# 16-head cross attention: the scores of four heads on four quarters of TensorE's rows

## The chip, the cores and the metric

The kernel runs on one core of a Trainium2 chip. The metric is the device time of one execution in microseconds (us), lower is better. TensorE is PE in the profile (its weight loads are PEld), VectorE is DVE, ScalarE is ACT, GpSimd is POOL, and SP issues most DMAs.

## The reference

A decoder of four layers, each of them self attention, cross attention and feed-forward, in float32, on x of 8 batches x 100 rows x 256 channels. Three of the four cross attentions (layers 0, 1 and 3) have 16 heads of 16 channels and attend to a context of 361 rows. Cut to what matters:

```python
def _L3_xattn_ref(x, context, Wq, Wk, Wv, Wo, bo):      # 16 heads of 16 channels
    q = (x @ Wq.T).reshape(B, Qlen, HEADS, HEAD_DIM).transpose(0, 2, 1, 3)
    k = (context @ Wk.T).reshape(B, KVlen, HEADS, HEAD_DIM).transpose(0, 2, 1, 3)
    v = (context @ Wv.T).reshape(B, KVlen, HEADS, HEAD_DIM).transpose(0, 2, 1, 3)
    scores = jnp.einsum('bhqd,bhkd->bhqk', q, k) / scale
    attn = jax.nn.softmax(scores, axis=-1)
    out = jnp.einsum('bhqk,bhkd->bhqd', attn, v)
    ...
    return out @ Wo.T + bo
```

Layer 0 adds biases, rotary embedding and a key mask, layer 1 biases and a gate on the values.

## The kernel before

`build` emits the sublayers one after another with a barrier of all engines between them. `cross_attn16` is called three times: as `l0x` (with rotation and key mask), `l1x` (with the gate) and `l3x`. Tiles carry that prefix (`l1x_pr`). Layer 2 has another function with four heads, which is not touched.

A stage of `cross_attn16` first projects keys, values and queries of all batches. `kt` holds the keys transposed: 128 partitions are 8 heads of 16 channels, and the 16 heads fill two such blocks (`KC = 2`). Then comes the score loop over 32 quads (8 batches x 4 quads of 4 heads), written out by hand on every engine; the order in the code is the order of each engine's queue:

- PE, step n: transposes of heads 0 and 1 of quad n-1 (`turn`, L1078); the scores of quad n (`score`, L1068), one PSUM bank of `wide` for each head; transposes of heads 2 and 3 of quad n-1; in every fourth step, each at another place, one of `back` (L1098), `turn_y` (L1104), `project_y` (L1110), which finish a batch; then the product with the values of quad n-2 (`weigh`, L1089).
- DVE, step n: copy of head 0 of quad n-1 out of PSUM (`copy_pt`, L1340); the lowest score of each row for quad n (`lowest`): in l1x and l3x two reduces over two heads each (L1356), in l0x one pass for each head that also adds the mask (L1350); copy of head 2 of quad n-1; in some steps `divide` or `add`.
- ACT, step n: copy of head 1 of quad n-1 (L1200), exponentials of heads 0 and 1 of quad n (L1209), copy of head 3 of quad n-1, exponentials of heads 2 and 3.

`turned` has two banks: the transposes of head 0 of quad n wait until the copy of head 2 of quad n-1 has read bank 0. Head i of a score waits until bank i of `wide` has been read: by ACT's exponential of the quad before (l1x, l3x), or by DVE's pass (l0x).

A head's 16 channels are fewer than the partitions that a matmul takes, so the queries are masked: POOL writes `qm` (L1250), which holds copies of the queries in which all channels but one head's are zero, for two batches by turns. Before, a head's score contracts 64 partitions, `t` chooses the half, and `qm` has four masked copies. The host permutes the columns of the query and key weights by `SLOT_HEAD`, so that the heads 0, 1, 2, 3 of a quad lie in the halves 0, 1, 0, 1.

The trace shows each float32 matmul as two weight loads and two matmuls: 128 head scores of a stage are 256 matmuls.

Of the kernel before, what the change touches and what calls it, by code (L numbers as in the profile page):

```python
# [17 lines left out]
B, S, E = 8, 100, 256  # L18
P = 128
KC = E // P  # L20
SKV = 361
# [8 lines left out]
ALU = mybir.AluOpType  # L30
# [884 lines left out]
                walk(dve, front, step, finish)  # L915


SLOT_HEAD = [8 * m + 4 * (j // 2) + 2 * (j % 2) + t for m in range(KC) for t in range(2) for j in range(4)]


@sublayer
def cross_attn16(net, name, rope=False, biases=False, key_mask=False, gate=False, load=False):
# [3 lines left out]
    nc, dram = net.nc, net.dram  # L926
# [6 lines left out]
    with ExitStack() as ctx:  # L933
        def sb(n, shape, dt=F32):
            return ctx.enter_context(nc.sbuf_tensor(name + "_" + n, shape, dt))

        w = {n: sb(n, [P, KC, E]) for n in ("wk", "wv", "wq", "wo")}
        pairs = [(w["wk"][:], dram[name + "_wk"])]
# [8 lines left out]
        if rope:  # L947
# [2 lines left out]
            pairs += [(swap[:], dram["rope_swap"]), (cos[:], dram["rope_cos"]), (sin[:], dram["rope_sin"])]  # L950
            kraw, qraw = sb("kraw", [P, 2, KC, SKV]), sb("qraw", [P, KC, HALF * S])
            ksin, qsin = sb("ksin", [P, KC, SKV]), sb("qsin", [P, KC, HALF * S])
        headmask = sb("headmask", [P, 4])
        pairs += [(w["wq"][:], dram[name + "_wq"]), (headmask[:], dram["headmask4"]), (w["wo"][:], dram[name + "_wo"])]
        bo = None
        if name + "_bo" in dram:
            bo = sb("bo", [S, E])
# [7 lines left out]
        xn = sb("xn", [S, B, E])  # L965
        xt = sb("xt", [P, KC, B, S])
        qt = sb("qt", [P, KC, B, S])
        qm = sb("qm", [P, 2, KC, 4, S])
        kt = sb("kt", [P, B, KC, SKV])
        v1 = sb("v1", [CH, B, NCH, H, V])  # L970
        nmx = sb("nmx", [S, 2, Q])
# [15 lines left out]
        wide, turned, summed, side = net.wide, net.turned, net.summed[:, 0, :], net.summed[:, 1, :]  # L987
# [19 lines left out]

        def rows_of(c):
            return CH if c < NCH - 1 else LAST

        def slot_of(g, i):
            return g // 2, i % 2, 2 * (g % 2) + i // 2

        with nc.Block() as block:
            @block.sync
            def _(sp):
                load_weights(sp, net, pairs[:1], sem["loaded"])
                if load:
                    net.context.load(sp, net)
                load_weights(sp, net, pairs[1:], sem["loaded"])  # L1020

            @block.tensor
            def _(pe):
# [36 lines left out]
                def score(n):  # L1060
                    b, g = n // NQ, n % NQ
                    if g == 0:
                        pe.wait_ge(sem["qm_ready"], b + 1)
                    for i in range(Q):
                        m, t, j = slot_of(g, i)
                        if n >= 1:
                            pe.wait_ge(sem["m_ready" if key_mask else "p_ready"], Q * (n - 1) + i + 1)
                        pe.matmul(wide[0:S, i, 0:SKV], qm[64 * t:64 * t + 64, b % 2, m, j, :], kt[64 * t:64 * t + 64, b, m, :],  # L1068
                                  start=True, stop=True).then_inc(sem["s_psum"], 1)

                def turn(n, heads):
# [69 lines left out]
                for n in range(QUADS + 2):  # L1141
                    if 1 <= n <= QUADS:
                        turn(n - 1, (0, 1))
                    if n < QUADS:
                        score(n)
                    if 1 <= n <= QUADS:
                        turn(n - 1, (2, 3))
                    b = n // NQ - 1
                    if n % NQ == 2 and b >= 0:
                        back(b)  # L1150
                    elif n % NQ == 3 and b >= 0:
                        turn_y(b)
                    elif n % NQ == 0 and b >= 1:
                        project_y(b - 1)
                    if n >= 2:
                        weigh(n - 2)
# [81 lines left out]
            @block.gpsimd  # L1238
            def _(pool):
                pool.memset(pr[:, :, SKV:PADKV], 0.0).then_inc(sem["pad_ready"], 1)  # L1240
                pool.memset(v1[:, :, :, :, D:V], 0.0)
                pool.drain()
                pool.memset(v1[:, :, :, :, D:D + 1], 1.0).then_inc(sem["ones_ready"], 1)
                pool.wait_ge(sem["loaded"], n_loaded)
                for b in range(B):
                    pool.wait_ge(sem["q_ready"], KC * (b // HALF) + KC)
                    if b >= 2:
                        pool.wait_ge(sem["s_psum"], H * (b - 1))
                    for m in range(KC):
                        last = pool.tensor_tensor(qm[:, b % 2, m], qt[:, m, b, :].unsqueeze(1).broadcast_to([P, 4, S]),  # L1250
                                                  headmask[:].unsqueeze(2).broadcast_to([P, 4, S]), ALU.mult)
                    last.then_inc(sem["qm_ready"], 1)

            @block.vector
# [1763 lines left out]
def build(nc, dram):  # L3018
    with ExitStack() as ctx:
        net = Net(nc, ctx, dram)  # L3020
        with ExitStack() as kept:
            net.context = Context(net, kept, "ctxt")
            front(net)
        l3_attn(net)
        net.context = Context(net, ctx, "ctxt3")
        cross_attn16(net, "l3x", load=True)
        l3_ffn(net)
        store(net)


def front(net):
    setup(net)
    l0_attn(net)
    cross_attn16(net, "l0x", rope=True, biases=True, key_mask=True)
    l0_ffn(net)
    l1_attn(net)
    cross_attn16(net, "l1x", biases=True, gate=True)
    l1_ffn(net)
    l2_attn(net)
    cross_attn(net, "l2x", 4, mask=("query_mask", U8))  # L3040
    l2_ffn(net)


def _layouts(a):

    def wide(w):
        return w.reshape(-1, P, w.shape[-1]).transpose(1, 0, 2)

    def col(b):
        return b.reshape(-1, P).T  # L3050

    d = {"x": a["x"], "ident": np.eye(P, dtype=np.float32)}
    d["causal"] = np.where(np.arange(S)[:, None] < np.arange(S)[None, :], np.float32(NEG), np.float32(0))
    d["ctxt"] = a["ctx_1024"].transpose(0, 2, 1).reshape(B, KC, P, SKV).transpose(0, 2, 1, 3)
    for D in (16, 64):
        d[f"headmask{D}"] = (np.arange(P)[:, None] // D == np.arange(P // D)[None, :]).astype(np.float32)
    d["headmask4"] = ((np.arange(P)[:, None] % 64) // 16 == np.arange(4)[None, :]).astype(np.float32)
    slots = (np.array(SLOT_HEAD)[:, None] * 16 + np.arange(16)[None, :]).reshape(-1)
    for n in ("q", "k", "v"):
        d["l0a_w" + n] = wide(a["L0_attn_w_" + n].reshape(-1, E).T)  # L3060
    d["l0a_wo"] = wide(a["L0_attn_w_o"])
    for k, n in (("l0x", "L0_xattn"), ("l1x", "L1_xattn")):
        for m in "qkvo":
            d[f"{k}_w{m}"] = wide(a[f"{n}_W{m}"][:, slots] if m in "qk" else a[f"{n}_W{m}"])
        for m in "qk":
            d[f"{k}_b{m}"] = col(a[f"{n}_b{m}"][slots])
        for m in "vo":
            d[f"{k}_b{m}"] = a[f"{n}_b{m}"]
    wkv = a["L2_xattn_Wkv"]
    for m, w in (("q", a["L2_xattn_Wq"]), ("k", wkv[:E]), ("v", wkv[E:]), ("o", a["L2_xattn_Wout"])):  # L3070
        d["l2x_w" + m] = wide(w.T)
    for m in "qkvo":
        d["l3x_w" + m] = wide(a["L3_xattn_W" + m].T[:, slots] if m in "qk" else a["L3_xattn_W" + m].T)
    d["l3x_bo"] = a["L3_xattn_bo"]
    d["key_mask"] = a["mask_Bx1x1xS2_if1"].reshape(B, SKV)
    bits = np.zeros((B, S, -(-SKV // 4) * 4), np.bool_)
    bits[:, :, 0:SKV] = a["mask_BxSxS2_bk0"]
    d["query_mask"] = bits.view(np.int32)

    D = 16  # L3080
    r = np.arange(P) % D
    inv = (1.0 / np.float32(10000.0) ** (np.arange(0, D, 2, dtype=np.float32) / np.float32(D))).astype(np.float32)
    angle = (np.arange(SKV, dtype=np.float32)[None, :] * inv[r % (D // 2)][:, None]).astype(np.float32)
    d["rope_cos"], d["rope_sin"] = np.cos(angle), np.sin(angle)
    swap = np.zeros((P, P), np.float32)
    for p in range(P):
        lower = r[p] < D // 2
        swap[p + D // 2 if lower else p - D // 2, p] = -1.0 if lower else 1.0
    d["rope_swap"] = swap

    rows = np.minimum(np.arange(PADKV), SKV - 1)
    d["energy"] = a["ctxb_2048x8"][:, rows].reshape(B * NCH, CH, 8).transpose(1, 0, 2)
    more_layouts(a, d, wide, col)
    return {k: np.ascontiguousarray(v) for k, v in d.items()}
# [13 lines left out]
```

## Time and profile before

| | |
|---|---|
| three runs | 2272.12, 2280.46, 2282.67 us; median 2280.46 us |
| the profiled execution | 2281.18 us, span of its instructions 2279.2 us |
| mean granted clock of TensorE | 0.846 |
| score loop of l0x, first to last score | 175.5 us |
| score loop of l1x, first to last score | 129.8 us |
| score loop of l3x, first to last score | 127.7 us |

The span is the time from the first to the last instruction; the execution's own time is 2.0 us longer. The three score loops together are 433.0 us of 2279.2 us; all else in the kernel is not touched by the change, apart from the size of one small weight tile and of the masked queries. A granted clock of 1.00 is 2.4 GHz and 0.50 is 1.2 GHz; values between are means over a stretch in which both levels occur.

### The profile page before, as it was taken

Reading aid. Unit: us, or ns where it says so; the run is one execution under the profiler, and the core shown is the slowest. Engines: PE = TensorE matmul, PEld = TensorE weight load, DVE = VectorE, ACT = ScalarE, POOL = GpSimd, SP = SyncE. Lnnn points to the kernel's source line nnn. Section 1 sums busy time; section 2 is a strip of 40 time slices with the busy share of each in tenths; the row PEclk is TensorE's granted clock in tenths of the full one; section 3 lists DMA queues with packets and bytes.
Section 4 is the critical chain, followed back from the end, with each engine's and each line's share of the span. In section 5 each row is a group of like instructions: output and inputs, shape, how many; then the busy total and the mean of one; then the engine's idle time right before and its main releaser. Section 6 shows DMA issues by size and latency. Waiting matters only on the chain. (4 is left out here: it accounts for less than half of the span.)

```text
span 2279.2 us, 30680 instructions
## 1 busy us (share of the span) xinstructions
PE 1711.9 (75%) x10556; PEld 1224.0 (54%) x10556; DVE 1069.9 (47%) x2341; ACT 728.8 (32%) x1482; POOL 331.8 (15%) x247
## 2 busy tenths in 40 slices
PE   4998688779789799879996177728925572199978
PEld 4887455546478566568885055517712220066643
DVE  2544465655543457520000623320028899736665
ACT  1222135543288256422221122212213300026630
POOL 0000100000021101031112100020022994101000
PEclk9999798988855899889998578958968775599989
DMA  3000100001000000143653100044120000100010
GB/s 142 1 0 6 46 1 1 1 9 35 26 1 0 25 1 2 63 146 114 209 190 111 43 22 14 7 176 149 55 68 0 0 0 0 73 0 2 2 45 15
DMA packets 41358, 102.73 MB, mean 45 GB/s; under 512 B 9789, under 2 KB 27690, under 8 KB 36404
## 3 DMA queue, kind: packets, MB, share of 16 engines
q1 hardware_dynamic: 29194, 56.85, 7.2%
q0 software_dynamic: 7216, 39.63, 5.2%
q10 hardware_dynamic: 4830, 4.71, 0.7%
q8 instruction: 70, 1.15, 0.2%
q14 instruction: 48, 0.39, 0.1%
HBM read 89.28 MB, written 11.88 MB: 44 GB/s over the span
## 5 line engine op out<-in xcount | busy, mean ns | idle before, releaser
L2602 PE MATMUL wide<-l3a_qk,ident 100*100 100x512 f32 x144 | 80.3, 714 | 51.1 <-POOL l3a_qk L2692 50.3
L2030 PE MATMUL summed<-l1f_pack,l1f_hidden 128*100 128x256 f32 x480 | 107.3, 382 | 2.9 <-ACT l1f_hidden L2079 2.9
L2164 DVE TENSOR_TENSOR l1f_out<-summed,l1f_b 100x512 f32<-100x512 f32 x15 | 10.4, 692 | 187.8 <-PE summed L2030 187.8
L2030 PEld LDWEIGHTS summed<-l1f_pack,l1f_hidden 128*100 128x100 f32 x480 | 78.9, 167 | 27.9 <-ACT l1f_hidden L2079 5.9
L1209 ACT ACTIVATE l0x_pr<-l0x_sc,l0x_nmx 100x361 f32<-100x361 f32 x128 | 75.1, 593 | 56.8 <-DVEq L1352 55.9
L1350 DVE CUSTOM_DVE_ANT_0 l0x_sc<-wide,l0x_words 100x361 f32<-100x361 f32 x128 | 68.4, 534 | 50.6 <-PE wide L1068 33.2
L2079 ACT ACTIVATE l1f_hidden<-wide,l1f_pack 128x200 f32<-128x200 f32 x120 | 48.9, 426 | 135.0 <-PE wide L2024 82.8
L1078 PE MATMUL turned<-ident,l0x_pr 100*121 100x100 f32 x384 | 62.8, 305 | 35.5 <-DVE l0x_pt L1340 22.3
L2692 POOL TENSOR_TENSOR l3a_qk<-l3a_cw,l3a_score 100x1024 f32<-100x1024 f32 x36 | 86.6, 2438 | 4.3 <-DVE l3a_score L2756 4.3
L1078 PEld LDWEIGHTS turned<-ident,l0x_pr 100*121 100x121 f32 x384 | 52.0, 208 | 63.9 <-ACT l0x_pr L1209 42.3
L2024 PE MATMUL wide<-l1f_rt,l1f_pack 128*128 128x200 f32 x480 | 83.9, 333 | 0.7 <-ACT l1f_rt L2089 0.7
L2024 PEld LDWEIGHTS wide<-l1f_rt,l1f_pack 128*128 128x128 f32 x480 | 81.6, 190 | 2.4 <-issue 1.5
L2602 PEld LDWEIGHTS wide<-l3a_qk,ident 100*100 100x100 f32 x144 | 27.1, 198 | 102.5 <-POOL l3a_qk L2692 55.4
L1209 ACT ACTIVATE l1x_pr<-wide,l1x_nmx 100x361 f32<-100x361 f32 x128 | 65.2, 567 | 47.1 <-DVE l1x_nmx L1356 47.1
L1209 ACT ACTIVATE l3x_pr<-wide,l3x_nmx 100x361 f32<-100x361 f32 x128 | 65.1, 567 | 44.7 <-DVE l3x_nmx L1356 44.7
L1356 DVE TENSOR_REDUCE l1x_nmx<-wide 100x2 f32<-100x722 f32 x64 | 55.4, 905 | 26.3 <-PE wide L1068 26.3
L1356 DVE TENSOR_REDUCE l3x_nmx<-wide 100x2 f32<-100x722 f32 x64 | 55.3, 905 | 24.3 <-PE wide L1068 24.3
L1068 PE MATMUL wide<-l0x_kt,l0x_qm 64*100 64x361 f32 x256 | 58.4, 584 | 5.2 <-DVE l0x_kt L1290 5.2
L1078 PEld LDWEIGHTS turned<-ident,l1x_pr 100*121 100x121 f32 x384 | 46.3, 187 | 29.6 <-issue 17.9
L1078 PEld LDWEIGHTS turned<-ident,l3x_pr 100*121 100x121 f32 x384 | 45.5, 184 | 29.3 <-issue 17.5
L1078 PE MATMUL turned<-ident,l1x_pr 100*121 100x100 f32 x384 | 56.5, 284 | 5.9 <-DVE l1x_pt L1340 5.4
L1078 PE MATMUL turned<-ident,l3x_pr 100*121 100x100 f32 x384 | 55.8, 281 | 6.7 <-DVE l3x_pt L1340 5.6
(523 smaller groups left out, 3931.6 us busy)
## 6 DMA issues: line engine op xcount, KB each, us to landing
l2f_w<-l2f_w_dram SPq DMA_DIRECT2D x16, 1024.0 KB
ctxt<-ctxt_dram SPq DMA_DIRECT2D x4, 1083.0 KB, 8.1
l1f_sorted_x<-l1f_zeros SPq DMA_DIRECT2D x15, 200.0 KB
l1f_rows<-l1f_sorted_x SPq DMA_DIRECT2D x15, 200.0 KB
l1f_sorted_y<-l1f_out ACTq DMA_DIRECT2D x15, 200.0 KB
l2x_ctxt<-ctxt_dram SPq DMA_DIRECT2D x8, 361.0 KB
l0f_w<-l0f_w_dram SPq DMA_DIRECT2D x18, 128.0 KB
l1f_shared<-l1f_shared_dram SPq DMA_DIRECT2D x1, 2052.0 KB
```

Source lines behind the costliest of these rows:

```text
L1068: pe.matmul(wide[0:S, i, 0:SKV], qm[64 * t:64 * t + 64, b % 2, m, j, :], kt[64 * t:64 * t + 64, b, m, :], start=True, stop=True).then_inc( ...
L1078: last = pe.transpose(turned[0:CH, i % 2, c * S:(c + 1) * S], pr[:, h % 8, c * CH:(c + 1) * CH], net.ident[0:S, 0:S])
L1209: act.activation(pr[:, h % 8, 0:SKV], src, ACT.Exp, bias=nmx[:, n % 2, i:i + 1], scale=-1.0).then_inc(sem["p_ready"], 1)
L1350: dve.tensor_tensor_reduce(sc[:, i, :], wide[0:S, i, 0:SKV], bias[:, b, :], 1.0, 3e38, ALU.add, ALU.min, nmx[:, n % 2, i:i + 1])
L1356: dve.tensor_reduce(nmx[:, n % 2, 2 * pair:2 * pair + 2], wide[0:S, 2 * pair:2 * pair + 2, 0:SKV], X_AX, ALU.min).then_inc(sem["m_ready"], 2)
L2024: last = pe.matmul(wide[:, f % 4, 0:CR], w1_of(w, k, f), cols(k), start=k == 0, stop=k == KC - 1)
L2030: last = pe.matmul(banks[0:S, c, 0:E], hidden[:, f, c * S:(c + 1) * S], w2_of(w, f), start=f == 0, stop=f == FC - 1)
L2079: act.activation(hidden[:, f, :], wide[:, f % 4, 0:CR], ACT.Gelu, bias=b1_of(w, f)).then_inc(read, 1)
L2164: dve.tensor_tensor(out[:, slot], summed[0:S, :, 0:E], b2[:, slot, :].unsqueeze(1).broadcast_to([S, RT, E]), ALU.add).then_inc(sem["y_read ...
L2602: last = pe.matmul(wide[0:S, 2 * (t % 2) + half, :], net.ident[0:S, 0:S], ring[:, n % RING, half * HALF:(half + 1) * HALF], start=u == 0, ...
L2692: pool.tensor_tensor(ring[:, n % RING, :].rearrange("s (h c) -> s h c", h=H), cw[:, u, :].rearrange("s (h c) -> s h c", h=H), score[:, n, ...
```

## The change

The scores of the four heads of a quad are placed on four quarters of the array's rows. A head's score now contracts 32 partitions (two heads' channels), heads 0 to 3 of a quad take the partitions 0-31, 32-63, 64-95 and 96-127, and the masked queries need two copies instead of four. `SLOT_HEAD`, the host's permutation, follows. Number, order, waits and increments of PE's instructions stay as they are; so do the output banks.

```diff
-SLOT_HEAD = [8 * m + 4 * (j // 2) + 2 * (j % 2) + t for m in range(KC) for t in range(2) for j in range(4)]
+SLOT_HEAD = [8 * m + 4 * t + i for m in range(KC) for i in range(4) for t in range(2)]
...
-        headmask = sb("headmask", [P, 4])
-        pairs += [(w["wq"][:], dram[name + "_wq"]), (headmask[:], dram["headmask4"]), (w["wo"][:], dram[name + "_wo"])]
+        headmask = sb("headmask", [P, 2])
+        pairs += [(w["wq"][:], dram[name + "_wq"]), (headmask[:], dram["headmask2"]), (w["wo"][:], dram[name + "_wo"])]
...
-        qm = sb("qm", [P, 2, KC, 4, S])
+        qm = sb("qm", [P, 2, KC, 2, S])
...
-        def slot_of(g, i):
-            return g // 2, i % 2, 2 * (g % 2) + i // 2
...
-                        m, t, j = slot_of(g, i)
                         if n >= 1:
                             pe.wait_ge(sem["m_ready" if key_mask else "p_ready"], Q * (n - 1) + i + 1)
-                        pe.matmul(wide[0:S, i, 0:SKV], qm[64 * t:64 * t + 64, b % 2, m, j, :], kt[64 * t:64 * t + 64, b, m, :],
+                        pe.matmul(wide[0:S, i, 0:SKV], qm[32 * i:32 * i + 32, b % 2, g // 2, g % 2, :], kt[32 * i:32 * i + 32, b, g // 2, :],
                                   start=True, stop=True).then_inc(sem["s_psum"], 1)
...
-                        last = pool.tensor_tensor(qm[:, b % 2, m], qt[:, m, b, :].unsqueeze(1).broadcast_to([P, 4, S]),
-                                                  headmask[:].unsqueeze(2).broadcast_to([P, 4, S]), ALU.mult)
+                        last = pool.tensor_tensor(qm[:, b % 2, m], qt[:, m, b, :].unsqueeze(1).broadcast_to([P, 2, S]),
+                                                  headmask[:].unsqueeze(2).broadcast_to([P, 2, S]), ALU.mult)
...
-    d["headmask4"] = ((np.arange(P)[:, None] % 64) // 16 == np.arange(4)[None, :]).astype(np.float32)
+    d["headmask2"] = ((np.arange(P)[:, None] % 32) // 16 == np.arange(2)[None, :]).astype(np.float32)
```

## Rows read from the trace of the kernel before

**Rows 1.** The page of the whole execution: span, then busy time (share) x instructions of each engine.

```profile
span 2279.2 us, 30680 instructions
...
PE 1711.9 (75%) x10556; PEld 1224.0 (54%) x10556; DVE 1069.9 (47%) x2341; ACT 728.8 (32%) x1482; POOL 331.8 (15%) x247
```

**Rows 2.** Stretches: score loops of l0x, l1x, l3x. Length, busy (x) of PE, PEld, DVE, ACT, POOL, PEclk.

```profile
317.70:493.20 175.50, 141.59 (x1376) 93.98 (x1376) 105.53 (x336) 96.49 (x197) 9.98 (x12) 0.88 0.01 2
808.70:938.50 129.80, 124.37 (x1376) 84.12 (x1376) 88.59 (x149) 84.01 (x197) 9.98 (x12) 0.97 0.01 2
2040.80:2168.50 127.70, 121.48 (x1374) 82.83 (x1374) 88.38 (x149) 83.67 (x197) 9.98 (x12) 1.00 0.01 2
```

**Rows 3.** Groups by line, score loop of l1x: busy us, mean ns, idle before and releaser.

```profile
L1356 DVE TENSOR_REDUCE l1x_nmx<-wide 100x2 f32<-100x722 f32 x64 | 55.4, 905 | 26.3 <-PE wide L1068 26.3
L1068 PE MATMUL wide<-l1x_kt,l1x_qm 64*100 64x361 f32 x256 | 48.8, 501 | 2.5 <-issue 2.5
...
L1250 POOL TENSOR_TENSOR l1x_qm<-l1x_qt,l1x_headmask 128x400 f32<-128x400 f32 x12 | 10.0, 852 | 115.9 <-PE wide L1068 115.9
```

**Rows 4.** Timeline of l1x, PE, two quads: start us, us, what, count, idle before.

```profile
859.16 1.46 PE L1068 MATMUL wide<-l1x_kt,l1x_qm 64*100 64x361 f32 x8
...
861.26 1.03 PE L1110 MATMUL summed<-l1x_wo,l1x_yt 128*100 128x256 f32 x4
...
863.68 1.46 PE L1068 MATMUL wide<-l1x_kt,l1x_qm 64*100 64x361 f32 x8
865.07 0.88 PE L1078 MATMUL turned<-ident,l1x_pr 100*121 100x100 f32 x6
865.88 0.72 PE L1089 MATMUL summed<-l1x_pt,l1x_v 121*32 121x100 f32 x24
866.93 0.85 PE L1078 MATMUL turned<-ident,l1x_pr 100*121 100x100 f32 x6 [0.33 <-DVE l1x_pt L1340]
867.71 0.55 PE L1068 MATMUL wide<-l1x_kt,l1x_qm 64*100 64x361 f32 x2
```

**Rows 5.** Timeline of l1x, DVE, the quad from 863.68.

```profile
864.68 1.73 DVE L1356 TENSOR_REDUCE l1x_nmx<-wide 100x2 f32<-100x722 f32 x2 [0.73 <-PE wide L1068]
866.32 0.46 DVE L1340 COPY l1x_pt<-turned 121x300 f32<-121x300 f32 x1
```

**Rows 6.** Timeline of l1x, ACT, the quad from 863.68.

```profile
865.62 1.01 ACT L1209 ACTIVATE l1x_pr<-wide,l1x_nmx 100x361 f32<-100x361 f32 x2 [1.42 <-DVE l1x_nmx L1356]
...
866.83 1.02 ACT L1209 ACTIVATE l1x_pr<-wide,l1x_nmx 100x361 f32<-100x361 f32 x2
```

**Rows 7.** Timeline of PE cut down to 863.8 to 864.0, then to 864.10 to 864.15.

```profile
863.68 0.55 PE L1068 MATMUL wide<-l1x_kt,l1x_qm 64*100 64x361 f32 x2
...
863.68 0.85 PE L1068 MATMUL wide<-l1x_kt,l1x_qm 64*100 64x361 f32 x4
```

**Rows 8.** Timeline of l0x, PE, the end of the quad from 392.00.

```profile
396.65 0.85 PE L1078 MATMUL turned<-ident,l0x_pr 100*121 100x100 f32 x6 [1.72 <-DVE l0x_pt L1340]
397.42 0.55 PE L1068 MATMUL wide<-l0x_kt,l0x_qm 64*100 64x361 f32 x2
```

**Rows 9.** Timeline of l0x, DVE, the quad from 392.00: first head, last copy.

```profile
392.99 0.53 DVE L1350 CUSTOM_DVE_ANT_0 l0x_sc<-wide,l0x_words 100x361 f32<-100x361 f32 x1 [0.73 <-PE wide L1068]
...
396.03 0.47 DVE L1340 COPY l0x_pt<-turned 121x300 f32<-121x300 f32 x1 [0.19 <-issue]
```

**Rows 10.** Stretches: two of l0x, then two quads of l1x; columns as in rows 2.

```profile
420.20:423.40 3.20, 3.20 (x22) 2.16 (x22) 2.33 (x9) 2.14 (x5) 0.00 (x0) 0.50 0.00 0
389.50:420.00 30.50, 23.35 (x273) 15.98 (x273) 19.03 (x62) 17.81 (x37) 1.66 (x2) 1.00 0.00 1
812.89:817.98 5.09, 4.54 (x21) 2.63 (x21) 2.41 (x4) 2.84 (x7) 0.00 (x0) 0.69 0.00 0
867.71:871.80 4.09, 4.09 (x49) 2.87 (x48) 3.15 (x7) 3.00 (x8) 0.00 (x0) 1.00 0.02 4
```

**Rows 11.** Timeline of l1x, DVE, second reduce of the quad from 812.89.

```profile
815.77 0.91 DVE L1356 TENSOR_REDUCE l1x_nmx<-wide 100x2 f32<-100x722 f32 x1 [0.29 <-PE wide L1068]
```

## The prediction, made before the changed kernel ran

> **What bounds the kernel now.** I read the page first: PE is busy for 75% of the span and DVE for 47%, but that is a mean over twelve sublayers [rows 1]. So I cut out the three stretches that the change touches, first to last score of each stage [rows 2]. PE is busy for 121.48 of 127.70 us in l3x (95%), for 124.37 of 129.80 in l1x, for 141.59 of 175.50 in l0x. By that alone PE bounds l1x and l3x, and the score matmuls, 48.8 us there [rows 3], are a third of it. But a stretch that is nearly full of PE work can still be set by a loop through other engines, so the next view is the timeline of one quad.
>
> In l1x the quad that begins at 863.68 lasts until 867.71, 4.03 us [rows 4]. Most quads of l1x and l3x last that long. PE has one pause in it: 0.33 us before the transposes at 866.93, and what ends it is DVE's copy of line 1340, not a score. Followed back on DVE [rows 5]: the copy runs from 866.32 to 866.78, directly behind two reduces that start at 864.68 and hold DVE for 1.73 us; these start when the scores of heads 0 and 1 are there, 1.00 us after the first score. So the loop is: score begins, +1.00 first reduce, about +2.64 copy of head 2, about +3.25 next transposes of heads 0 and 1, about +4.03 next score. Nothing in it asks when heads 2 and 3 are scored: they are needed by the second reduce alone, which starts some 0.82 us after the first (864.68 + 1.73 - 0.91, with 905 ns a reduce [rows 3]), at +1.82. The scores have all ended by +1.46.
>
> Two of four quads have more PE work and no pause. The one from 859.16 has the output projection of 1.03 us and lasts 4.52 us [rows 4]; there are six of these in each of l1x and l3x. The one from 867.71 has the transposes of line 1098 and lasts 4.09 us with PE busy for all of it [rows 10]; seven in each. Only in these does PE set the time.
>
> In l0x a quad takes 397.42 - 392.00 = 5.42 us at full clock, PE pauses for up to 1.72 us, again ended by the copy of line 1340 [rows 8], and DVE is in four single passes from 392.99 to the copy at 396.03 [rows 9]. The loop has the same form, with a longer DVE part.
>
> **The change part by part.** *The scores.* Cut to a narrow window, the trace has two matmuls in flight at 863.8, and four that span 0.85 us when the second passes have begun [rows 7]: the halves of the rows really work at once, and two heads take 0.85 us. The whole quad takes 1.46, so the second pair of heads adds 0.61. If four quarters work at once, as two halves do, the quad takes 0.85 us: PE gains 0.61 us in each of 96 quads, 58.6 us of PE time. No row shows four row quarters. The nearest are the products of line 1089, where four heads lie on four quarters of the columns: 24 matmuls in 0.72 us, 30 ns each [rows 4], where six transposes of the same 100 columns on the whole array take 0.88 us, 147 ns each. So four small matmuls at once are usual for this array, and I take 0.85. The bounds are 1.46 (still by pairs) and, as the worst, four that share what two have now, so that all four end at 1.46 and heads 0 and 1 too.
>
> Where does the 0.61 go? In the usual quad it becomes pause. Heads 0 and 1 are ready at +0.85 as before, the reduces start at +1.00, and every later step of the loop stays. Gain: nothing; the cover is the loop through DVE. In the quads in which PE sets the time the gain is cut by two things. One is the loop's 4.03 us. The other is a wait that so far is hidden: heads 2 and 3 wait for ACT to have read their banks. ACT's last exponential of the quad ends at 866.83 + 1.02 = 867.85 [rows 6], 0.14 us after the next score has begun; with the step to PE I put heads 2 and 3 at +0.2 at the earliest. Before they began at +0.69, so it cost nothing; now the scores end at about 1.05, and PE gains 0.41. The quad with the projection goes from 4.52 to 4.11: 6 x 0.41 = 2.5 us a stage. The other goes from 4.09 to the loop's 4.03: 7 x 0.06 = 0.4 us. That is 2.9 us a stage, 5.8 us for l1x and l3x. Behind the waiting score of head 2 stand the transposes of heads 2 and 3 and the values' product; nobody waits for these before the next transposes at +3.25. A single case more: in the first two quads of l1x the clock is partly at 1.2 GHz, the second reduce waits for the scores, 0.29 us [rows 11], and that goes: 0.6 us for two. Sum so far: -6.4 us.
>
> In l0x the scores of heads 2 and 3 are wanted still later, since DVE takes heads one by one, and no quad at full clock is set by PE. Gain: nothing.
>
> *The masked queries.* POOL's multiplication, 852 ns each, has half the elements. POOL waits for PE 115.9 us in the loop of l1x [rows 3], so this is worth nothing, and would be worth nothing if it were slower. The smaller mask's DMA and the permuted weights change no wait.
>
> *The clock.* This is the only part that can cost. In l0x the mean granted clock is 0.88 [rows 2], so a share of 2 x 0.12 = 0.24 of the 175.5 us, 42 us, is at 1.2 GHz; one such stretch stands in [rows 10]. What PE did before it fell was pausing. The stage has 31 quads from first to last score; at 5.42 us they would be 168.0, it is 175.5, so the lower level costs 7.5 us, 0.18 for each us at it. The change adds 0.61 us of pause to every quad of l0x, some 19 us in all. I take 20 us more at the lower level, x 0.18 = 3.6 us; the bounds are none, and twice as much as now, 7.5 us. That four heads at once shorten slow quads in which PE is full works against it; at most all 7.5 us of today come back. In l1x and l3x the pause grows too: PE would be busy for about 121.48 - 32 x 0.41 = 108.4 of 125 us in l3x, 13% idle. The long stretch of l0x from 389.50 to 420.00 has PE idle for 7.15 of 30.50 us, 23%, and stays at 2.4 GHz throughout [rows 10]. By that row l1x and l3x keep their clock, and I take nothing. The Trainium skill says (TensorE: Matmul & The Clock Gate, Part 1) that the gate follows how busy the array has been lately, which is a rule against this change: a faster score leaves the array idle more. The trace agrees in l0x, and whether the rule bites in l1x and l3x is the first rival below.
>
> Sum: -5.8 - 0.6 + 3.6 = -2.8 us. The profiled execution took 2281.18 us (span 2279.2 and 2.0 around it), which lies 0.7 above the median of the three runs. 2281.18 - 2.8 = 2278.4; I say 2278.
>
> **The rivals.** *The clock falls in l1x and l3x as well (slower).* Place: the score loops of both. For it: pauses grow from 0.33 to over 0.7 us in the usual quad, and l0x shows that pauses bring the clock down. Against: the row with 23% idle. Price: the l1x quad from 812.89 lasted 5.09 us at a mean clock of 0.69 [rows 10], which is 0.62 of it or 3.2 us at the lower level, for 1.06 us more than 4.03: 0.34 a us. If both loops spend a quarter of their 257 us there, as l0x does, it is 64 x 0.34 = 22 us, with 7.5 in l0x and -6.4: +23, 2304 us. It decides from about 50 us at the lower level in the two.
>
> *The four quarters share, and the first heads come late (slower).* Heads 0 and 1 end at 1.46 and no longer at 0.85; each loop gets 0.61 longer, 96 x 0.61 = 58.6 us, 2340 us. Against: halves do not slow each other, column quarters do not.
>
> *The array still takes them two at a time.* Nothing but POOL's work changes: 2281 us.
>
> *PE is the bound after all.* 96 x 0.61 us come off, 2223 us. For it: 95% busy in l3x. Against: the pause ended by DVE's copy in the usual quads. The Trainium skill (TensorEngine Tiling (Array Packing), PSUM Bottleneck) warns that a faster TensorE can leave the copies out of PSUM as the limit, and the trace agrees that DVE, which reads these scores, is already in the loop.
>
> *l0x gets its slow quads back.* The clock does not fall oftener there, and the 7.5 us of excess come off with the 6.4: 2267 us.
>
> **How the numbers follow.** Chances: the forecast 0.64, clock in l1x and l3x 0.12, shared quarters 0.05, pairs as before 0.06, PE the bound 0.05, l0x back 0.08. The forecast's own range is 2271 to 2288: all the bounds of its terms (-6.4 with -7.5 is the last rival; -6.4 with +7.5 is 2282, and the three runs spread by 10 us). To leave out no more than 2 in 10, the range goes to the clock rival above and to the l0x rival below: 2266 to 2304. A change within 0.5%, 11.4 us, is about what a measurement of this kernel cannot tell from none; the forecast and the pairs fall there (0.70), slower are the clock and the sharing (0.17), faster PE as bound and l0x (0.13).
>
> **What would show it.** The scores of a quad span 0.85 to 1.05 us and no longer 1.46. In l1x and l3x the first reduce still starts 1.00 us after the score, usual quads stay at 4.03 us, and PE's pause before the transposes grows to 0.7 to 0.9 us, ended by the copy of line 1340. The projection's quad takes 4.1 us. The loops last about 126 us (l1x) and 125 us (l3x), that of l0x 179 us at a clock near 0.83. I am wrong if the first reduce starts later or earlier than +1.00, if the clock of l1x or l3x is under 0.95, or if usual quads are shorter than 4.0 us.

## The result, and the profile after

The changed kernel takes 2300.8 us (median of five runs, 2294.95 to 2309.5), the kernel before 2280.46 us: ratio 1.0093, 95% interval 1.006 to 1.0126. It is slower, by about 20 us. The time lies inside the range that the prediction gave, but the prediction said "no change", and a small gain at that; what happened comes nearest to its first rival, the clock that falls in l1x and l3x too, though not for that rival's reason nor in its sizes. A second measurement gave 1.0090 (1.0058 to 1.0122). One of the nine executions of l0x_whole below, 3577 us at a granted clock of 0.975 against 2251 to 2261 us of the other eight, is in a slow state and is left out of its ratio.

First the page of the changed kernel, then its three score loops (l0x, l1x, l3x, first to last score; columns as in [rows 2]):

```profile
span 2298.8 us, 30680 instructions
...
PE 1711.9 (74%) x10556; PEld 1236.0 (54%) x10556; DVE 1067.5 (46%) x2341; ACT 729.5 (32%) x1482; POOL 316.2 (14%) x247
...
PEclk9999877777855779889998578959968775598979
```

```profile
315.90:503.30 187.40, 149.45 (x1377) 103.14 (x1378) 105.26 (x336) 96.43 (x197) 6.00 (x12) 0.70 0.01 1
820.00:952.40 132.40, 118.92 (x1377) 84.65 (x1377) 87.62 (x149) 83.85 (x197) 6.00 (x12) 0.90 0.01 2
2053.90:2187.00 133.10, 120.95 (x1375) 85.82 (x1375) 87.65 (x149) 83.94 (x197) 6.00 (x12) 0.88 0.01 2
```

PE's busy time is the same to a tenth, 1711.9 us, and that is the first hint: the scores need less of it at full clock, so the rest must have become slower. The loops went from 175.5 to 187.4, from 129.8 to 132.4 and from 127.7 to 133.1 us, 19.9 us together, and the span grew by 19.6: all of it is there. The granted clock went from 0.88 to 0.70, from 0.97 to 0.90 and from 1.00 to 0.88.

Where the clock is at 2.4 GHz, the trace does what the prediction said. PE in l1x, a quad with the projection and the usual quad behind it, which answer to [rows 4]:

```profile
858.93 1.05 PE L1064 MATMUL wide<-l1x_kt,l1x_qm 32*100 32x361 f32 x8
...
860.62 1.03 PE L1106 MATMUL summed<-l1x_wo,l1x_yt 128*100 128x256 f32 x4
...
863.04 0.96 PE L1064 MATMUL wide<-l1x_kt,l1x_qm 32*100 32x361 f32 x8
863.93 0.88 PE L1074 MATMUL turned<-ident,l1x_pr 100*121 100x100 f32 x6
864.74 0.72 PE L1085 MATMUL summed<-l1x_pt,l1x_v 121*32 121x100 f32 x24
866.29 0.85 PE L1074 MATMUL turned<-ident,l1x_pr 100*121 100x100 f32 x6 [0.83 <-DVE l1x_pt L1336]
867.07 0.56 PE L1064 MATMUL wide<-l1x_kt,l1x_qm 32*100 32x361 f32 x3
```

The scores take 1.05 and 0.96 us (before 1.46). The projection's quad lasts 863.04 - 858.93 = 4.11 us (before 4.52), the usual one 4.03 us as before, and PE's pause before the transposes grew from 0.33 to 0.83 us, still ended by DVE's copy. DVE shows why, as in [rows 5]:

```profile
864.04 1.73 DVE L1352 TENSOR_REDUCE l1x_nmx<-wide 100x2 f32<-100x722 f32 x2 [0.73 <-PE wide L1064]
865.68 0.46 DVE L1336 COPY l1x_pt<-turned 121x300 f32<-121x300 f32 x1
```

The reduces start at 864.04, 1.00 us behind the first score, exactly as before. Scoring heads 2 and 3 earlier gives the loop nothing.

What the prediction did not have is this. Three stretches of the loop of l3x, then one of l1x and one of l0x:

```profile
2053.90:2058.10 4.20, 2.54 (x21) 1.55 (x22) 2.20 (x3) 2.23 (x5) 0.00 (x0) 1.00 0.00 0
2058.30:2088.80 30.50, 30.32 (x225) 21.17 (x227) 15.46 (x25) 15.63 (x36) 1.00 (x2) 0.50 0.01 2
2089.00:2187.00 98.00, 87.70 (x1135) 62.92 (x1123) 69.79 (x121) 65.88 (x157) 5.00 (x10) 1.00 0.01 2
823.00:849.50 26.50, 25.59 (x184) 17.69 (x187) 12.45 (x20) 12.69 (x30) 1.00 (x2) 0.50 0.00 1
315.94:360.40 44.46, 35.51 (x258) 24.17 (x258) 22.69 (x72) 20.67 (x41) 1.00 (x2) 0.52 0.01 1
```

l3x begins at 2.4 GHz, PE is busy for 2.54 of the first 4.20 us, and then 30.5 us are at 1.2 GHz, after which the clock comes back and stays. In the kernel before, the loop of l3x is at 2.4 GHz throughout. l1x has 26.5 us of the same, and the first 44.46 us of l0x have a mean clock of 0.52, so nearly all of them are at 1.2 GHz, there with pauses of PE. One of the slow quads of l3x, PE and then the first reduce on DVE:

```profile
2067.62 1.54 PE L1064 MATMUL wide<-l3x_kt,l3x_qm 32*100 32x361 f32 x8
2069.09 1.54 PE L1074 MATMUL turned<-ident,l3x_pr 100*121 100x100 f32 x6
2070.56 1.23 PE L1085 MATMUL summed<-l3x_pt,l3x_v 121*32 121x100 f32 x24
2071.72 1.54 PE L1074 MATMUL turned<-ident,l3x_pr 100*121 100x100 f32 x6
2073.20 0.94 PE L1064 MATMUL wide<-l3x_kt,l3x_qm 32*100 32x361 f32 x4
```

```profile
2069.29 1.73 DVE L1352 TENSOR_REDUCE l3x_nmx<-wide 100x2 f32<-100x722 f32 x2 [1.70 <-PE wide L1064]
```

The quad lasts 5.58 us, PE has no pause at all in it, and yet the clock stays down for some five such quads. In the kernel before, the quad from 812.89 in l1x was at the lower level too [rows 10], but the clock was back before its end. Why a PE without a pause didn't get its clock back is what the experiments had to explain.

### The profile page after: what moved, and what is told of

It reads as the page before. It is cut to its first block and busy times, and to the rows that moved or that the text cites. A ratio compares the mean times of both kernels' runs of the same rounds, so it can differ in the third digit from the quotient of the medians.

```text
span 2298.8 us, 30680 instructions
## 1 busy us (share of the span) xinstructions
PE 1711.9 (74%) x10556; PEld 1236.0 (54%) x10556; DVE 1067.5 (46%) x2341; ACT 729.5 (32%) x1482; POOL 316.2 (14%) x247
## 5 line engine op out<-in xcount | busy, mean ns | idle before, releaser
L1074 PE MATMUL turned<-ident,l0x_pr 100*121 100x100 f32 x384 | 76.8, 354 | 40.3 <-DVE l0x_pt L1336 24.5
L1074 PEld LDWEIGHTS turned<-ident,l0x_pr 100*121 100x121 f32 x384 | 64.2, 251 | 73.7 <-ACT l0x_pr L1205 48.8
L2160 DVE TENSOR_TENSOR l1f_out<-summed,l1f_b 100x512 f32<-100x512 f32 x15 | 10.4, 692 | 187.4 <-PE summed L2026 187.4
L1074 PEld LDWEIGHTS turned<-ident,l3x_pr 100*121 100x121 f32 x384 | 52.0, 207 | 39.3 <-issue 21.6
L1074 PEld LDWEIGHTS turned<-ident,l1x_pr 100*121 100x121 f32 x384 | 51.3, 205 | 40.1 <-issue 21.0
L1074 PE MATMUL turned<-ident,l1x_pr 100*121 100x100 f32 x384 | 62.2, 303 | 14.3 <-DVE l1x_pt L1336 12.6
L1074 PE MATMUL turned<-ident,l3x_pr 100*121 100x100 f32 x384 | 63.0, 306 | 13.1 <-DVE l3x_pt L1336 11.4
L2885 PE MATMUL wide<-l3f_we,l3f_xt 128*100 128x512 f32 x128 | 59.7, 621 | 1.2 <-DVE l3f_acc L2953 1.2
```

The source lines that it names most:

```text
L1074: last = pe.transpose(turned[0:CH, i % 2, c * S:(c + 1) * S], pr[:, h % 8, c * CH:(c + 1) * CH], net.ident[0:S, 0:S])
L2160: dve.tensor_tensor(out[:, slot], summed[0:S, :, 0:E], b2[:, slot, :].unsqueeze(1).broadcast_to([S, RT, E]), ALU.add).then_inc(sem["y_read ...
L2885: last = pe.matmul(wide[0:S, n, :], xt[:, k, b, :], we[:, k, n * 512:(n + 1) * 512], start=k == 0, stop=k == KC - 1)
```

## The experiments

Each kernel ran on one chip together with the kernel before, whose median was between 2263 and 2282 us from chip to chip; so ratios to the kernel before are what to compare. The three numbers of us are the score loops of one profiled execution, from the start of the first score to the start of the last, with the granted clock. Some expectations count to the end of the last score, 0.3 to 0.9 us more, and 2.0 us more where scores use 128 rows.

| kernel | ratio (95%) | l0x | l1x | l3x |
|---|---|---|---|---|
| before | 1 | 175.5 (0.88) | 129.8 (0.97) | 127.7 (1.00) |
| changed | 1.0093 (1.006 to 1.0126) | 187.4 (0.70) | 132.4 (0.90) | 133.1 (0.88) |
| changed_again | 1.0090 (1.0058 to 1.0122) | 190.3 (0.67) | 127.6 (0.96) | 133.1 (0.88) |
| fill_start | 1.0051 (1.0034 to 1.0067) | 187.2 (0.71) | 127.9 (0.98) | 124.7 (1.00) |
| fill_start_32 | 1.0144 (1.0116 to 1.0172) | 189.5 (0.68) | 135.7 (0.89) | 135.3 (0.89) |
| fill_128 | 0.9953 (0.9933 to 0.9973) | 170.6 (0.97) | 126.5 (0.99) | 124.7 (1.00) |
| fill_32 | 1.0497 (1.0468 to 1.0526) | 250.0 (0.54) | 144.7 (0.85) | 149.1 (0.82) |
| two_quarters | 1.0285 (1.0259 to 1.0312) | 202.5 (0.64) | 144.3 (0.86) | 151.1 (0.81) |
| l0x_quarters_only | 1.0084 (1.0063 to 1.0105) | 190.0 (0.67) | 132.0 (0.95) | 127.7 (1.00) |
| l0x_whole | 0.9955 (0.9936 to 0.9974) | 164.0 (0.99) | 132.0 (0.95) | 127.7 (1.00) |
| halves_fill | 0.9949 (0.9932 to 0.9966) | 170.1 (0.98) | 128.1 (1.00) | 127.8 (1.00) |
| whole_and_quarters | 0.9976 (0.9957 to 0.9995) | 164.1 (0.99) | 135.4 (0.86) | 133.1 (0.88) |
| l0x_whole_quarters | 0.9903 (0.9882 to 0.9924) | 164.2 (0.99) | 125.0 (1.00) | 124.6 (1.00) |

**Is it the clock? Dummies in the first quads.** `fill` emits dummy matmuls into columns of PSUM that nothing else uses, ahead of `weigh`; each is two instructions on the PE. They change no result.

```diff
+def fillers(name, n):
+    return {0: 8, 1: 6, 2: 3}.get(n, 0) if name != "l0x" else 0
...
+                def fill(n):
+                    for _ in range(fillers(name, n)):
+                        pe.matmul(summed[:, NQ * S:512], net.ident[0:128, :], ctxt[0:128, 0, 0, 0:512 - NQ * S], start=True, stop=True)
...
+                    fill(n)
                     if n >= 2:
                         weigh(n - 2)
```

> The changed kernel with dummy matmuls (two instructions of 112 columns each, whole array, into unused columns) in the first three steps of the score loops of l1x and l3x alone: 8, 6 and 3 of them. Clock theory: in the changed kernel both loops begin with some 27 and 31 us at 1.2 GHz, because PE pauses in the first quads; with the pauses filled the clock stays at 2.4 GHz, l1x goes from 132.4 to about 126 us, l3x from 133.1 to about 125 us, and the whole is about 14 us faster than the changed kernel: 2287 us. Rival (the four row quarters cost time by themselves, the clock is a by-product): the dummies change nothing or cost 2 to 4 us, 2301 to 2305 us. l0x stays at about 187 us in either.

Loops of fill_start:

```profile
312.40:499.60 187.20, 148.19 (x1374) 102.30 (x1374) 105.19 (x336) 96.38 (x197) 5.98 (x12) 0.71 0.01 1
815.20:943.10 127.90, 114.55 (x1411) 83.34 (x1411) 87.55 (x149) 83.53 (x197) 5.98 (x12) 0.98 0.01 2
2029.60:2154.30 124.70, 111.92 (x1411) 81.31 (x1411) 87.55 (x149) 83.44 (x197) 5.98 (x12) 1.00 0.01 2
```

PE executes 34 instructions more in each of l1x and l3x, and l3x gets 8.4 us shorter, 124.7 us; l1x goes to 127.9. The changed kernel and this one differ by 0.42% of the whole, 9 to 10 us; 14 were expected, of which 13 show in the profile. The intervals of the two ratios, 1.006 to 1.0126 and 1.0034 to 1.0067, just touch, so this pair alone doesn't settle the time of the whole; the last pair of kernels below does. In l3x the long slow stretch is no cost that four quarters have by themselves: with quarters and dummies the loop has none. The first quads of a stage have few or no transposes and products of earlier quads to do, and the stretch doesn't come when dummies on the whole array stand in for them. l0x is as slow as in the changed kernel, as expected.

**Dummies everywhere, on 128 rows and on 32.** 3 to 6 dummies in a step of l0x (8 in the first), up to 3 in a usual step of l1x and l3x; the second kernel is the same but for the rows.

```diff
-                        pe.matmul(summed[:, NQ * S:512], net.ident[0:128, :], ctxt[0:128, 0, 0, 0:512 - NQ * S], start=True, stop=True)
+                        pe.matmul(summed[:, NQ * S:512], net.ident[0:32, :], ctxt[0:32, 0, 0, 0:512 - NQ * S], start=True, stop=True)
```

> The changed kernel with dummy matmuls on the whole array in the pauses of all three score loops: 3 to 8 in a step of l0x, up to 3 in a usual step of l1x and l3x, more in their first steps. Clock theory: no stretch at 1.2 GHz in l1x and l3x (126 and 125 us), and few in l0x, whose quads go to their 5.42 us: 168 to 172 us instead of 187. Whole: 2265 to 2275 us, faster than both kernels. Rival (quarters cost by themselves): 2300 us or more, since the dummies only add work.

> As the kernel with dummies in all pauses, with the same number of dummies, columns and instructions, but each contracts 32 partitions and not 128. If the clock goes by how long the array is kept busy, whatever part of it works, this is as fast as the one with 128: 2265 to 2275 us. If it goes by how many rows of the array work, the dummies are worth a quarter: the clock stays low as in the changed kernel, and the dummies stretch the slow quads of l0x: 2295 to 2315 us.

Loops of fill_128, then of fill_32:

```profile
318.40:489.00 170.60, 143.52 (x1696) 112.90 (x1696) 104.83 (x336) 96.58 (x197) 5.98 (x12) 0.97 0.01 2
802.50:929.00 126.50, 123.58 (x1500) 93.27 (x1500) 87.54 (x149) 83.61 (x197) 5.99 (x12) 0.99 0.01 2
2014.00:2138.70 124.70, 122.36 (x1503) 92.20 (x1503) 87.60 (x149) 83.56 (x197) 5.99 (x12) 1.00 0.01 2
```

```profile
318.20:568.20 250.00, 247.60 (x1696) 187.44 (x1696) 105.64 (x336) 96.98 (x197) 5.99 (x12) 0.54 0.00 1
887.60:1032.30 144.70, 144.30 (x1500) 106.75 (x1500) 87.62 (x149) 84.27 (x197) 5.98 (x12) 0.85 0.01 2
2116.00:2265.10 149.10, 149.00 (x1500) 109.36 (x1500) 87.75 (x149) 84.35 (x197) 5.99 (x12) 0.82 0.01 2
```

The two execute the same number of instructions with the same columns. With 128 rows the kernel is faster than the one before by 0.47%, and l0x has a clock of 0.97. With 32 rows it is 5% slower, and in l0x PE is busy for 247.60 of 250.00 us at 1.2 GHz for nearly all of it (0.54). By PE's busy time the second kernel is the busiest of all, and it has the lowest clock. Of the size I had expected less, 1.006 to 1.015: I had not thought that l0x would stay down for the whole loop, where the dummies themselves take twice as long.

That objection, dummies that lengthen quads which are already slow, doesn't apply if they stand in the first three steps alone, before the clock falls:

> As the kernel with dummies in the first three steps of l1x and l3x alone, but each dummy contracts 32 partitions. It lies in pauses before the clock has fallen, so that it can't be blamed for lengthening slow quads as the dummies of 32 rows in all pauses could. If the clock goes by rows: the loops of l1x and l3x begin at 1.2 GHz as in the changed kernel, 132 to 136 us each, ratio 1.008 to 1.014. If by busy time alone: 128.4 and 125.1 us as with whole-array dummies, ratio 1.005.

```profile
826.30:962.00 135.70, 124.80 (x1408) 90.38 (x1408) 87.53 (x149) 83.75 (x197) 6.00 (x12) 0.89 0.01 2
2064.40:2199.70 135.30, 125.00 (x1408) 90.14 (x1408) 87.64 (x149) 83.81 (x197) 6.00 (x12) 0.89 0.01 2
```

Both loops have about the clock of the changed kernel and are 3.3 and 2.2 us longer than in it; the ratio, 1.0144, is at the upper end of what was expected. The first 6.9 us of the loop of l3x in three kernels, the one before, fill_start and fill_start_32, and then what follows in the third:

```profile
2040.80:2047.70 6.90, 4.84 (x30) 2.97 (x30) 4.30 (x6) 3.71 (x9) 0.00 (x0) 1.00 0.00 0
2029.60:2036.50 6.90, 6.90 (x58) 5.58 (x59) 4.30 (x6) 3.72 (x9) 0.00 (x0) 1.00 0.00 0
2064.40:2071.30 6.90, 6.90 (x56) 5.61 (x56) 4.30 (x6) 3.72 (x9) 0.00 (x0) 1.00 0.00 0
2071.50:2102.00 30.50, 30.50 (x232) 21.66 (x233) 13.55 (x22) 14.20 (x33) 1.00 (x2) 0.50 0.01 2
```

This is the cleanest comparison of all. Before the clock falls, PE is busy for all of the 6.90 us with either kind of dummy, and for only 4.84 us in the kernel before. With dummies of 32 rows the clock then falls and is down for 30.5 us in which PE has no pause; with dummies of 128 rows, and in the kernel before with its scores of 64 rows, it never falls in this loop. The dummies of 32 rows put the fall off, from 4.2 us after the first score in the changed kernel to 7, and don't prevent it. Between the two kernels with dummies only the dummies' rows differ. So PE's busy time doesn't decide: the clock followed how much of the array's rows worked.

**The scores themselves, with half the rows for the same time.** Heads 0 and 2 on one quarter, heads 1 and 3 on another: two scores run at a time, as with halves.

```diff
-SLOT_HEAD = [8 * m + 4 * t + i for m in range(KC) for i in range(4) for t in range(2)]
+SLOT_HEAD = [8 * m + 4 * (q // 2) + 2 * t + q % 2 for m in range(KC) for q in range(4) for t in range(2)]
...
-                        pe.matmul(wide[0:S, i, 0:SKV], qm[32 * i:32 * i + 32, b % 2, g // 2, g % 2, :], kt[32 * i:32 * i + 32, b, g // 2, :],
+                        q = 2 * (g % 2) + i % 2
+                        pe.matmul(wide[0:S, i, 0:SKV], qm[32 * q:32 * q + 32, b % 2, g // 2, i // 2, :], kt[32 * q:32 * q + 32, b, g // 2, :],
```

> Scores of 32 partitions as in the changed kernel, but heads 0 and 2 of a quad on one quarter of the rows and heads 1 and 3 on another, so that two work at a time: the array is busy with scores as long as in the kernel before (1.46 us a quad), with half the rows. If the clock goes by busy time alone, this is the kernel before again, 2280 us, mean clock 0.846. If it goes by rows, the clock is as low as in the changed kernel or lower and the quads in which PE sets the time are as long as before: 2300 to 2315 us, clock 0.81 to 0.82. The rival that something else in the change costs time (layout of heads, smaller masked queries) also expects about 2300 us, but then with the clock of the kernel before.

```profile
314.40:516.90 202.50, 188.56 (x1376) 124.77 (x1376) 106.14 (x336) 96.50 (x197) 5.99 (x12) 0.64 0.01 1
831.00:975.30 144.30, 140.01 (x1376) 94.53 (x1376) 89.08 (x149) 84.73 (x197) 5.98 (x12) 0.86 0.01 2
2064.70:2215.80 151.10, 147.30 (x1374) 98.99 (x1374) 89.23 (x149) 85.09 (x197) 5.99 (x12) 0.81 0.01 1
```

Against the kernel before, PE is busy longer and the clock is lower in every loop, 0.64, 0.86 and 0.81 against 0.88, 0.97 and 1.00: 2.85% slower, where I had expected 0.9 to 1.5%. In this kernel as in the changed one a head's 16 channels come with 16 zeroed ones, and with halves they come with 48. The zeros are useless arithmetic, but the clock was higher where they were worked through. The rows and columns of score work are the same here as in the changed kernel, and yet this one is slower still: a slow quad lasts longer, since two pairs of scores one after the other take longer than four scores at once.

```profile
2094.73:2101.50 6.77, 6.77 (x47) 4.46 (x46) 2.67 (x4) 3.15 (x7) 0.00 (x0) 0.50 0.01 2
```

It takes 6.77 us and no longer 5.58, with PE busy for all of it. The rival that something else in the change costs time, with the clock of the kernel before, is out: the clock isn't that of the kernel before.

**Where the cost is.** The change in l0x alone, by an edit that lets each stage choose 32, 64 or 128 rows a head (the host's permutation and the mask follow):

```diff
+ROWS = {'l0x': 32, 'l1x': 64, 'l3x': 64}
...
+                        r, j = {32: (32 * i, g % 2), 64: (64 * (i % 2), 2 * (g % 2) + i // 2), 128: (0, 4 * (g % 2) + i)}[R]
+                        pe.matmul(wide[0:S, i, 0:SKV], qm[r:r + R, b % 2, g // 2, j, :], kt[r:r + R, b, g // 2, :],
```

> The change in l0x alone, halves in l1x and l3x. If the cost is local to each stage, l0x takes about 188 us (110 us of it at 1.2 GHz) and l1x and l3x the 131 and 129 us of the kernel before: ratio 1.0045. If a slow stage also pulls the following ones down, l1x is over 131 us too.

l0x takes 190.0 us at a clock of 0.67, l1x and l3x 132.0 and 127.7 us. l3x, far behind, is as before to a tenth. l1x is at 132.0 here and in l0x_whole alike, so it isn't l0x's slowness that moves it from 129.8. The ratio, 1.0084, is well above the expected 1.0045 and nearly that of the whole change, 1.0093 and 1.0090: l0x pays most of the cost. What l1x and l3x add lies within the intervals, which are 0.2 to 0.3% wide to either side, so about zero and up to some us either way.

**The other way round: fewer heads at once.** The same edit with 128 rows in l0x and halves elsewhere:

> The kernel before, but in l0x alone each head's score contracts all 128 partitions (eight masked copies of the queries), one head at a time. PE works longer for the scores: 8 steps of 0.30 us and the latency, some 2.6 us a quad instead of 1.46, which fits into its pause of up to 1.7 us and delivers head after head faster than DVE's 0.77 us a head. Rows theory of the clock: the array is fuller, the 44 us at 1.2 GHz in l0x go to under 10, its loop takes 169 to 171 us instead of 177, ratio to the kernel before about 0.997. Rival (only the time PE is busy with small matmuls matters, or packing heads is what keeps l0x short): the loop gets longer by the second head's later score, up to 0.3 us a quad, ratio 1.002 to 1.005.

```profile
318.30:482.30 164.00, 149.63 (x1374) 104.04 (x1375) 105.04 (x336) 96.74 (x197) 18.02 (x12) 0.99 0.01 2
```

```profile
386.62 2.59 PE L1071 MATMUL wide<-l0x_kt,l0x_qm 128*100 128x361 f32 x8
...
391.19 0.85 PE L1081 MATMUL turned<-ident,l0x_pr 100*121 100x100 f32 x6 [0.71 <-DVE l0x_pt L1343]
391.88 2.59 PE L1071 MATMUL wide<-l0x_kt,l0x_qm 128*100 128x361 f32 x8
```

```profile
392.80 0.54 DVE L1353 CUSTOM_DVE_ANT_0 l0x_sc<-wide,l0x_words 100x361 f32<-100x361 f32 x1 [0.57 <-PE wide L1071]
```

The scores of a quad take 2.59 us instead of 1.46, and l0x is 11.5 us shorter, 164.0 us at a clock of 0.99, also shorter than the 169 to 171 us expected; the kernel is 0.45% faster than the one before. The loop is even shorter than 31 quads of 5.42 us, 168.0. A usual quad lasts 391.88 - 386.62 = 5.26 us here, against 5.42 before. 0.08 of these 0.16 us go before the score: it starts 391.88 - 391.19 = 0.69 us after the transposes of heads 0 and 1 have begun, and in the kernel before 397.42 - 396.65 = 0.77 us [rows 8]. Another 0.07 us go behind it: the first pass on DVE starts 392.80 - 391.88 = 0.92 us after the score, and before 392.99 - 392.00 = 0.99 us [rows 9]. Over 31 quads that is some 5 of the 11.5 us; the rest goes with the slow stretches, of which 0.99 leaves next to none. PE is also busy for more of the loop here, 149.63 of 164.0 us against 141.59 of 175.5, so by itself this run doesn't tell rows from busy time.

**What quarters are worth with the clock held.**

> The kernel before (halves) with dummies on the whole array in PE's smaller pauses: up to 4 in a step of l0x, 1 in a usual step of l1x and l3x with a pause. What quarters are worth once the clock is held: with dummies, quarters took 171.0, 127.1 and 125.3 us. Halves should take 170 to 172, 128 and 128.5 (the quads with the projection stay at 4.52 us): ratio 0.996 to 0.998, 3 to 5 us slower than quarters with dummies. Rival (quarters themselves cost): halves with dummies are the faster of the two.

Halves with dummies: 170.1, 128.1 and 127.8 us. Quarters with dummies were 3.1 us shorter in l3x and 1.6 in l1x in the profile, and 0.5 longer in l0x, but the ratios of the whole, 0.9949 and 0.9953, don't tell them apart, where 3 to 5 us had been expected; the number of dummies differs too. Shown is that dummies help the kernel before too; that quarters beat halves under dummies isn't shown in the time of the whole. In l3x alone the table shows it time after time: wherever the loop is at 2.4 GHz throughout, it takes 127.7 or 127.8 us with halves (four kernels) and 124.6 or 124.7 us with quarters (three).

**Together.** Whole rows in l0x and quarters elsewhere, first without and then with the dummies of fill_start:

> Scores on the whole array in l0x, quarters in l1x and l3x, and no dummies at all. l0x 166 us as before with whole rows; if the fall at the start of l1x and l3x comes from their own first quads and not from anything that l0x leaves behind, both begin at 1.2 GHz as in the changed kernel, 131 to 134 us each, ratio 0.998 to 1.000, and the dummies of three steps are worth the whole way to 0.990. If not, 0.990 to 0.993 without dummies.

> Scores on the whole array in l0x, quarters in l1x and l3x with dummies in their first three steps. Rows theory: 169 to 171, 127 to 128.5 and 125.2 us, in sum 13 to 15 us less than the kernel before, ratio 0.993 to 0.995, as good as the kernel with dummies everywhere or better. Rival: l0x over 177 us, ratio 0.998 or more.

Loops of l0x_whole_quarters:

```profile
313.00:477.20 164.20, 149.84 (x1374) 104.20 (x1375) 105.02 (x336) 96.74 (x197) 18.02 (x12) 0.99 0.01 2
788.60:913.60 125.00, 111.97 (x1408) 81.34 (x1408) 87.51 (x149) 83.49 (x197) 5.99 (x12) 1.00 0.01 2
1999.40:2124.00 124.60, 111.93 (x1408) 81.34 (x1408) 87.50 (x149) 83.45 (x197) 6.00 (x12) 1.00 0.01 2
```

Without dummies l1x and l3x begin slow even behind a fast l0x: 135.4 and 133.1 us, the latter to a tenth that of the changed kernel. So the fall is the stage's own. With them they take 125.0 and 124.6 us, and the kernel is 0.97% faster than the one before, more than the 0.5 to 0.7% expected and the fastest of all; 413.8 us in the three loops instead of 433.0. These two kernels differ by the dummies of the first three steps alone, and their intervals, 0.9957 to 0.9995 and 0.9882 to 0.9924, lie apart: the dummies are worth 0.73% of the whole, some 17 us. changed_again was run beside whole_and_quarters to have both on one chip:

> The changed kernel once more, so that the two others have it on the same chip: ratio 1.007 to 1.011, l1x and l3x beginning with 20 to 31 us at 1.2 GHz.

It gave 1.0090; its l1x took 127.6 us at 0.96 instead of 132.4 at 0.90, so how long the slow start of l1x lasts differs from one execution to the next. Quarters without dummies have l1x at 132.4, 127.6 and 135.4 us and halves without dummies at 129.8, 132.0 and 132.0, so l1x by itself doesn't show what the change costs. l3x does: 133.1 us three times against 127.7 three times.

## Why the prediction was wrong, point by point

- **Four quarters work at once, 0.85 us a quad: right.** 1.05 and 0.96 us with the waits, 0.87 without (first quad of l3x in the changed kernel and in fill_start). The waits of heads 2 and 3 for ACT, taken as 0.2 us, are in the 1.05.
- **The usual quad gains nothing, since the loop runs through DVE: right.** 4.03 us before and after, first reduce at +1.00 in both, pause 0.83 us.
- **2.9 us of gain in each of l1x and l3x: right where the clock is up.** The projection's quad takes 4.11 us as worked out. fill_start has l3x at 124.7 us, which is 3.0 less than before, dummies included.
- **The smaller masked queries are worth nothing: not tested alone,** but no row contradicts it, and the 3.0 us of l3x leave little room for them.
- **The clock in l0x, "I take 20 us more at the lower level": the second step that failed, by its size.** 0.70 of 187.4 us is 112 us at 1.2 GHz against 42 before, 70 more. The price of 0.18 us for each of them was right: 11.9 us more for 70 us is 0.17. 3.6 us were forecast, 11.9 came, over the bound of 7.5 too: "twice as much as now" was no bound. That is 8.3 us of the miss. The 20 us were got from the added pause; fill_128 and fill_32 show that what fills the pause matters, and the first 44 us of the changed l0x are all but wholly at 1.2 GHz (0.52), which no term had.
- **The clock in l1x and l3x, "by that row l1x and l3x keep their clock, and I take nothing": the step that failed.** The clocks came in at 0.90 and 0.88, under the 0.95 named as a sign of being wrong. It cost 5.4 + 3.0 = 8.4 us in l3x; for l1x and l3x together -6.4 us were forecast and +8.0 measured in the profiled execution, 14.4 us of the miss. With the 8.3 of l0x that is 22.7 us, and 2278.4 + 22.7 is 2301 us, the measured time. The row behind the step was one of l0x with halves, where 23% pause did no harm; I compared pauses. The runs show that the pause is not the measure: fill_32 has next to none and the lowest clock, and fill_start_32 has none at the start of l3x and falls. Quarters take away half the score work of the array; and the first quads of l3x, which have little else, I had not looked at. Why the clock then stays down I read thus: at 1.2 GHz the same work stretches until PE has no pause, without filling more rows. The stretches of 30.5 us fit that; what ends them isn't shown.
- **The rival** had stages and direction right and was priced at 2304 us; I gave it 0.12. That 2300.8 us lies near is in part luck: it put 22 - 6.4 = 15.6 us on l1x and l3x, where 8.0 came, and 7.5 on l0x, where 11.9 came. Its reason, longer pauses in the usual quads, was wrong too: at 2.4 GHz these have the longer pause, 0.83 us, and keep the clock, and what fell were the first quads. Its weight should have been larger: that a clock falls where the array has less to do stood in the rows of l0x.

The Trainium skill says (TensorE: Matmul & The Clock Gate, Part 1) that the gate is set by how busy PE has been. The runs agree that work brings the clock up. They disagree if busy means the time in which PE has something to do: fill_128 and fill_32 differ in the dummies' rows alone, as do fill_start and fill_start_32, and the kernel before and two_quarters differ in rows and in where the heads lie.

What stays open: whether columns count as rows do, and which part of the array's state is looked at. Every dummy here had all 128 columns, and every dummy of 32 rows lay on the first quarter. Scores on 128 rows in l1x and l3x weren't tried.

## What to carry to other kernels

Before packing matmuls into fewer rows, ask two things of the trace: does anything wait for the packed result, and what is the clock in that stage. Where another engine sets the loop, a faster score only empties the array; in l0x, fuller matmuls with zeros in them cost nothing and kept nearly all of the loop at 2.4 GHz. Look at the first passes of a loop by themselves: in l3x that is where the pipeline was empty and the clock fell, and 17 dummy matmuls in each of two loops took 0.4% off the kernel in one pair of kernels and 0.7% in another, 10 to 17 us.

## What the runs showed of the hardware

- The granted clock followed how many rows of the array work, not PE's busy time: PE busy for 99% of l0x at a clock of 0.54 with dummies of 32 rows, for 84% at 0.97 with dummies of 128; and after 6.9 us in which PE was busy throughout in both, a fall with 32 rows and none with 128.
- A PE without pauses can stay at the lower clock: 30.5 us at 1.2 GHz in l3x of fill_start_32 with PE busy for all of them, and 30.32 us of 30.5 in the changed kernel.
- One head on 128 rows begins sooner than on a part of them: the score 0.69 instead of 0.77 us after the start of the transposes before it, the first pass on DVE at +0.92 instead of +0.99 us, and usual quads of l0x of 5.26 instead of 5.42 us. The Trainium skill states (TensorEngine Tiling (Array Packing), Key Properties) that a change of the tiling mode drains TensorE; by that statement scores on all rows would need no such change against the transposes around them, which contract 100 rows. The 0.16 us agree with that, and no run here isolates it.
